# Cross-attention with a routed FFN on one core: loads after the output products, bias masks inside the weight sums, a new order at each group's start, a new opening

## The reference, cut to what matters

```python
x = x + xattn(layernorm(x), ctx, mask, bias, Wq, Wk, Wv, Wo)    # 1024 tokens of 512
x = x + ffn(layernorm(x))                  # dense product plus 8 routed rank-16 experts

def xattn(hq, hkv, mask, bias, Wq, Wk, Wv, Wo):  # 16 batches of 64 tokens, 32 heads of 128
    q, k, v = hq @ Wq, hkv @ Wk, hkv @ Wv        # 512 -> 4096 each
    score = q @ k.T / sqrt(128) + bias           # per batch and head, 64 x 64
    probs = softmax(where(mask, score, -inf))
    return (probs @ v) @ Wo                      # 4096 -> 512
```

## Time and profile before

| | |
|---|---|
| device time, median of three runs | 797.49 us (796.79 to 798.37) |
| profiled execution | 799.1 us, span 797.3 us |
| TensorE clock granted | 1.000 of full speed over the whole span |
| PE busy | 98% of the span |
| DVE, ACT, POOL busy | 73%, 42%, 23% |
| DMA engines | 148 GB/s on average, of queue q1 46.7% of 16 engines |
| chain that ended last | PE 89%, DVE 7%, DMA 2%, issue 1%, SP queue 1% |

### The profile page before, as it was taken

One profiled execution on the slowest core, in us unless ns is written; L12 is line 12 of the kernel. 1 busy time (PEld: TensorE's weight loads), 2 busy tenths in 40 slices (PEclk: granted clock), 3 DMA queues, 4 the chain that ended last, 5 costly groups with the idle time before them and its releaser, 6 DMA issues.

```text
span 797.3 us, 16339 instructions
## 1 busy us (share of the span) xinstructions
PE 781.9 (98%) x6368; PEld 651.8 (82%) x6368; DVE 585.0 (73%) x1047; ACT 335.4 (42%) x657; POOL 186.6 (23%) x203
## 2 busy tenths in 40 slices
PE   9999999999999999989999999999999999999998
PEld 7788888888888888768888878887888788888886
DVE  6794626267677666688987888788878887869884
ACT  5563525245455555452443234423443343324420
POOL 0134041024334334242212221212221221010200
PEclk9999999999999999999999999999999999999999
DMA  6536674234544556583564355435543455344002
GB/s 224 196 121 211 214 238 145 106 142 159 186 163 159 164 165 211 168 245 107 159 186 114 103 163 179 126 105 159 170 144 114 141 160 167 93 121 101 1 3 105
DMA packets 108075, 118.35 MB, mean 148 GB/s; under 512 B 44240, under 2 KB 77008, under 8 KB 107999
## 3 DMA queue, kind: packets, MB, share of 16 engines
q1 hardware_dynamic: 107998, 117.31, 46.7%
HBM read 81.64 MB, written 35.65 MB: 147 GB/s over the span
## 4 chain that ended last, share of the span: by engine, by line
PE 89%; DVE 7%; DMA 2%; issue 1%; SPq 1%; ACT 0%; DVEq 0%
PE pY L1383 40%; PE pP L1383 36%; PE pY L1544 4%; PE pO L1569 2%; PE pT_ L1569 1%; DVE pr L1140 1%; DVE rs L1135 1%; DVE y L1101 1%; DVE sm L1131 1%; PE pO L1383 1%; PE pT_ L1554 1%; PE pS L1554 1%; DMA k_hbm<-stage 1%; DMA v<-v_hbm 1%; SPq L422 1%
## 5 line engine op out<-in xcount | busy, mean ns | idle before, releaser
L1383 PE MATMUL pY<-wo_hi,oT_hi 128*128 128x512 f32 x248 | 97.8, 394 | 3.6 <-DVE y L1101 2.3
L1101 DVE TENSOR_TENSOR y<-y,pY 128x512 f32<-128x512 f32 x124 | 84.7, 683 | 18.6 <-PE pY L1383 18.3
L1383 PE MATMUL pY<-wo_lo,oT_hi 128*128 128x512 f32 x248 | 96.7, 390 | 0.0
L1383 PE MATMUL pY<-wo_hi,oT_lo 128*128 128x512 f32 x248 | 96.6, 390 | 0.0
L1383 PE MATMUL pP<-xo_hi,wk_hi 128*128 128x512 f32 x210 | 83.7, 398 | 1.8 <-ACT v_s L633 0.8
L648 ACT CAST wk_hi<-twk 128x256 fp32r<-128x256 f32 x128 | 52.1, 408 | 72.6 <-PE pP L1383 61.1
L1383 PE MATMUL pP<-xo_lo,wk_hi 128*128 128x512 f32 x210 | 81.9, 390 | 0.0
L1383 PE MATMUL pP<-xo_hi,wk_lo 128*128 128x512 f32 x210 | 81.9, 390 | 0.0
L581 POOL TENSOR_TENSOR bias<-bias,madd 128x512 f32<-128x512 f32 x32 | 42.7, 1348 | 151.8 <-DMA bias<-in_fside_Bx32xSxS 151.8
L887 DVE TENSOR_TENSOR wk_lo<-twk,wk_hi 128x256 fp32r<-128x256 f32 x128 | 58.8, 464 | 23.3 <-ACT wk_hi L648 23.3
L887 DVE TENSOR_TENSOR wk_lo<-wk_raw,wk_hi 128x256 fp32r<-128x256 f32 x96 | 46.6, 486 | 21.9 <-ACT wk_hi L648 21.8
(11 more groups left out here) (277 smaller groups left out, 1916.9 us busy)
## 6 DMA issues: line engine op xcount, KB each, us to landing
v_hbm<-stage SPq DMA_DIRECT2D x64, 256.0 KB, 2.3
k_hbm<-stage SPq DMA_DIRECT2D x64, 256.0 KB, 3.5
k<-k_hbm SPq DMA_DIRECT2D x16, 1024.0 KB, 5.4
v<-v_hbm SPq DMA_DIRECT2D x16, 1024.0 KB, 7.3
wk_raw<-in_L_xattn_Wk SPq DMA_DIRECT2D x16, 512.0 KB, 4.4
wo_raw<-in_L_xattn_Wo SPq DMA_DIRECT2D x16, 512.0 KB, 3.7
bias<-in_fside_Bx32xSxS SPq DMA_DIRECT2D x128, 64.0 KB, 3.5
wk_raw<-in_L_xattn_Wq SPq DMA_DIRECT2D x16, 512.0 KB, 4.6
```

Source lines behind the costliest of these rows:

```text
L1101: nc.vector.tensor_tensor(y[:, t, :], y[:, t, :], src[:, :], ALU.add).then_inc(y_added, 1)
L1383: mm = nc.tensor.matmul(bank_, a, b, start=first and n == 0, stop=last and n == len(terms) - 1, skip_group_check=read_between)
```

## The change

1. **Opening.** In `ORDER` product 5 of block 1 goes before product 2 of block 2. Two ACT copies keep the transposed context tiles 0 and 4 in SBUF (`kept0`), so the eight transposes that made them again in block 5 are gone, with one ACT copy (`rows_out(0)`). On ACT `higher(0, 4)` goes ahead of `copy_u(1)`, and `sums_high(2)` ahead of `copy_v(1)`; on DVE `first_low(2)` goes after `first_t1` and `first_t4`, and `sums_low(2)` ahead of `make_c11(2)`.
2. **The turn from K to the groups.** At block QA ACT's `copy_c12` goes before the first `exp`, and DVE's `make_c11` before the first `weights`.
3. **SP.** In each group, in place of wo, k, bias, Q weights, [v products done] v: wo, [v products done] Q weights, bias, k, v.
4. **POOL.** The two masks stand between the third and the fourth weight sum, not after the fourth.
5. **ACT and DVE in a group.** `wo_high` goes ahead of `higher` 3, and `lower_wo` goes from behind the fifth `add_tile` to behind the second.
6. **PE in a group.** `scores(h + 2)`, `turn_p(h)`, `scores(h + 3)`, `turn_p(h + 1)`, then both `times_v`.
7. **Tail.** PE's `ffn_weights(6)` goes after the products with V, and ACT's two `o_high` go ahead of `split_ffn(6)`.

Line numbers in the changed kernel are 5 to 15 higher in places: L1397 is the product, L1115 `add_tile`, L896 `lower`, L561 the mask, L571 to L584 the sums, L1553, L1563 and L1578 scores, transposes and products with V.

```diff
@@ -81,7 +81,7 @@
-ORDER = [(1, 1), (0, 2), (1, 2), (0, 4), (0, 3), (0, 7), (1, 6), (1, 7), (2, 1), (2, 2), (1, 5), (1, 3), (2, 6),
+ORDER = [(1, 1), (0, 2), (1, 2), (0, 4), (0, 3), (0, 7), (1, 6), (1, 7), (2, 1), (1, 5), (2, 2), (1, 3), (2, 6),
          (2, 7), (1, 4), (2, 5)]
...
@@ -91,10 +91,9 @@
-FIRST_TURN = [0, 1, 4, 6, 10, 12, 14, 16]
-SECOND_TURN = [2, 3, 5, 7, 11, 13, 15, 17]
-AGAIN = (8, 9)
-NTURN = 18
+FIRST_TURN = [0, 1, 4, 6, 8, 10, 12, 14]
+SECOND_TURN = [2, 3, 5, 7, 9, 11, 13, 15]
+NTURN = 16
...
@@ -510,15 +511,16 @@
                 load_wo(i + 1)
+
+                sp.wait_ge(o_full, 4 * (i + 1))
+                if i + 24 < NSET:
+                    load_wk(i + 24)
                 if i + 2 < NP:
-                    sp.wait_ge(s_full, 2 * i + 4)
-                    load_k(i + 2)
                     for s in range(2):
                         sp.wait_ge(s_read, 2 * i + 3 + s)
                         load_bias(2 * i + 4 + s)
-                if i + 24 < NSET:
-                    load_wk(i + 24)
-                sp.wait_ge(o_full, 4 * (i + 1))
+                    sp.wait_ge(s_full, 2 * i + 4)
+                    load_k(i + 2)
                 load_v(i + 1)
...
@@ -553,7 +555,12 @@
                 nc.gpsimd.tensor_tensor(rstd[:, b:b + 1], ve[:, b:b + 1], mhalf[:, :], ALU.pow).then_inc(rstd_made, 1)
-            def sums_of_b(w):
+            def add_mask(h):
+                pool.wait_ge(ld_bias[h % 2], 64 * (h // 2 + 1))
+                b = bias[h % 2]
+                nc.gpsimd.tensor_tensor(b[:, :, :], b[:, :, :], madd[:, :, :], ALU.add).then_inc(bias_made, 1)
+
+            def sums_of_b(w, masks=()):
...
@@ -570,15 +577,12 @@
                 nc.gpsimd.tensor_tensor(tw[:, 2, :, :], raw_block(w, 0, 1), raw_block(w, 0, 0), ALU.subtract
                                         ).then_inc(tw_made, 1)
+                for h in masks:
+                    add_mask(h)
                 pool.wait_ge(w_lo[6], w)
...
                                         ).then_inc(tw_made, 1)
-
-            def add_mask(h):
-                pool.wait_ge(ld_bias[h % 2], 64 * (h // 2 + 1))
-                b = bias[h % 2]
-                nc.gpsimd.tensor_tensor(b[:, :, :], b[:, :, :], madd[:, :, :], ALU.add).then_inc(bias_made, 1)
...
@@ -594,11 +598,12 @@
             for i in range(NP):
+                heads = (2 * i + 2, 2 * i + 3) if i + 1 < NP else ()
                 if i + 22 < NSET:
-                    sums_of_b(i + 22)
-                if i + 1 < NP:
-                    add_mask(2 * i + 2)
-                    add_mask(2 * i + 3)
+                    sums_of_b(i + 22, heads)
+                else:
+                    for h in heads:
+                        add_mask(h)
             pool.wait_ge(ld_small, 48)
...
@@ -655,7 +660,7 @@
             def rows_out(j):
-                act.wait_ge(turned, AGAIN[1] + 1 if j == 0 else SECOND_TURN[j] + 1)
+                act.wait_ge(turned, SECOND_TURN[j] + 1)
                 if j != 1:
...
@@ -697,15 +702,21 @@
             piece_of_first(1, 3, pP[0], c12_made)
+
+            act.wait_ge(a21_l, 1)
+            nc.scalar.copy(kept0[0][:, :, :, :], first_turn(0)[:, :].rearrange("p (k c t) -> p k c t", k=2, c=2)
+                           ).then_inc(kept0_made, 1)
+            nc.scalar.copy(kept0[1][:, :, :], second_turn(0)[:, :].rearrange("p (c t) -> p c t", c=DC)
+                           ).then_inc(kept0_made, 1)
             piece_of_first(3, 7, pP[1], c22_made)
             first_high(2)
+            higher(0, 4)
             copy_u(1)
             rows_out(2)
             last_high(2)
-            higher(0, 4)
             copy_p1(2)
+            sums_high(2)
             copy_v(1)
-            sums_high(2)
             higher(0, 6)
...
@@ -736,8 +747,6 @@
                 if j is not None:
                     sums_high(j)
-                if n == 5:
-                    rows_out(0)
                 copy_v(n)
...
@@ -792,8 +801,8 @@
             copy_v(n)
             higher(w, 4)
+            copy_c12(n)
             exp(0)
-            copy_c12(n)
             higher(w, 5)
...
@@ -831,10 +840,10 @@
                 copy_u(n)
                 higher_of(w, 2)
+                wo_high(i + 1)
                 higher_of(w, 3)
                 copy_v(n)
                 higher_of(w, 4)
-                wo_high(i + 1)
                 copy_c12(n)
...
@@ -854,9 +863,9 @@
             turned_p(h + 3)
             split_ffn(5)
-            split_ffn(6)
             o_high(h + 2)
             o_high(h + 3)
+            split_ffn(6)
...
@@ -925,7 +934,12 @@
                 low_, s, k = low[j // 4], sums_a[j // 4], SUM_ORDER.index(j)
                 one = first_turn(j)[:, :].rearrange("p (k c t) -> p k c t", k=2, c=2)
-                dve.wait_ge(low_made, k + 1)
+                if j == 0:
+                    one, low_ = kept0
+                    dve.wait_ge(kept0_made, 2)
+                else:
+
+                    dve.wait_ge(low_made, k + 1 if j < 4 else k)
                 if k >= 1:
...
@@ -1029,13 +1043,13 @@
             lower_w(0, 2)
             make_c11(1)
-            first_low(2)
             first_t1()
             first_t4()
+            first_low(2)
             lower_w(0, 4)
             sums_of_a(2)
+            sums_low(2)
             make_c11(2)
-            sums_low(2)
             lower_w(0, 6)
...
@@ -1180,9 +1194,9 @@
             add_up(0)
             lower_w(w, 6)
+            make_c11(n)
             weights(0)
             lower_w(w2, 0)
-            make_c11(n)
             add_up(1)
...
@@ -1217,6 +1231,7 @@
                 weights(h + 3)
                 add_tile(i, 1)
+                lower_wo(i + 1)
                 lower_of(w, 1)
...
@@ -1226,7 +1241,6 @@
                 lower_of(w, 5)
                 add_tile(i, 4)
-                lower_wo(i + 1)
                 add_tile(i, 5)
...
@@ -1436,8 +1450,7 @@
                 if j == 2:
-                    pe.wait_ge(a6_lo, 1)
-                    pe.wait_ge(a21_l, 1)
+                    pe.wait_ge(kept0_made, 2)
                 elif j == 4:
...
@@ -1499,8 +1512,8 @@
             times(1, 7)
             times(2, 1)
+            times(1, 5)
             times(2, 2)
-            times(1, 5)
             times(1, 3)
...
@@ -1514,10 +1527,6 @@
                 if prep_at(n) is not None:
                     turn_pair(prep_at(n))
-                if n == 5:
-                    pe.wait_ge(a6_lo, 3)
-                    turn(ctx[:, 0, :], first_turn(0))
-                    turn(ctx[:, 4, :], second_turn(0))
                 times(n, 6)
...
@@ -1637,10 +1646,10 @@
                 n = QA + 2 + i
                 h = 2 * i
+                scores(h + 2)
                 turn_p(h)
+                scores(h + 3)
                 turn_p(h + 1)
-                scores(h + 2)
-                scores(h + 3)
                 times_v(h)
...
@@ -1677,9 +1686,9 @@
             turn_p(h + 3)
             ffn_weights(5)
-            ffn_weights(6)
             times_v(h + 2)
             times_v(h + 3)
+            ffn_weights(6)
...
```

More of the change, by code:

```diff
@@ L201, in xattn_ffn @@
         sums_a = [at("sums_c", R2 + 2048, [P, 4, 2, P]), at("sums_x", R4 + 8192, [P, 4, 2, P])]
+        kept0 = [at("kept0_a", R2 + 6144, [P, 2, 2, P]), at("kept0_b", R2 + 8192, [P, DC, P])]
         R5 = R4 + 24576
@@ L287, in xattn_ffn @@
         turned, turned_hi, turned_lo = sem("turned"), sem("turned_hi"), sem("turned_lo")
-        low_made, sum_step = sem("low_made"), sem("sum_step")
+        low_made, sum_step, kept0_made = sem("low_made"), sem("sum_step"), sem("kept0_made")
         a01_hi, a01_lo, a6_hi, a6_lo = sem("a01_hi"), sem("a01_lo"), sem("a6_hi"), sem("a6_lo")
@@ L474, in _ @@
                     for t in range(NT):
-                        sp.wait_ge(turned, 10)
+                        sp.wait_ge(turned, 8)
                         sp.dma_start(y[:, t, :], x_d[:, t, :]).then_inc(ld_x[t], 16)
@@ L987, in normalise @@
                     if m >= NX:
-                        dve.wait_ge(turned, 10 + m - NX + 1)
+                        dve.wait_ge(turned, 8 + m - NX + 1)
                     nc.vector.tensor_scalar(xn[:, b, :], y[:, t, :], mv[:, b, 0:1], rstd[:, b:b + 1],
```

## The result

The changed kernel takes 806.32 us (median of four runs, 804.75 to 811.61) against 797.22 (796.79 to 798.37): a ratio of 1.0124, 95% interval 1.0073 to 1.0174. It is 9.1 us slower. The forecast was 800.0, slower but by 2.5, with a range that ended at 805.

The account below looks back on a forecast made before the run. PE was taken as the bound, busy for 98% of the span. Terms -2.8 - 0.2 + 4.2 - 2.7 + 4.4 - 0.4 = +2.5, added to the median 797.5, gave 800.0 us, with a range of 793 to 805.

Parts of the forecast that it names:

- the price of PE's order in the groups: Start of each group on PE: more changes between kinds of matmul cost 0.32 us a group, +4.2 in 13 groups.
- this order is hidden in the first group: First group after K: the new order is hidden behind the load of v, so it costs nothing there.
- what the fetches give back: Products with V: gaps are late instruction fetches costing 4.6 us; moved block ends leave 1.9, so -2.7.
- The masks with the low part of wo and the fourth sum: Groups: POOL's port lock delays DVE, so wo2 or wo4 stops 0.7 us a group; 9.1 less 4.7, +4.4.
- The opening's two stops: Opening: PE's stops for the v_s copy and co_lo go, -1.6 us of the opening's -2.8.
- the two stops near 336 and 341: From K to the groups: both go, worth 1.3 us together, but v's load takes the time back; -0.2 taken.
- The tail's stop for the low part of o: Tail, before 740.00: ACT's casts of o now stand ahead of one cast of 0.5, so -0.4 us.
- nothing to buy: Groups: scores 1.6 us earlier gain nothing, since no row of PE waits for the bias, exp or pT.
- (b): Groups: two locks in each group stop PE 1.15 us a group, +10.3; total 805.9 us, chance 0.12.
- (c): Products with V: the gaps stay, 0 and not -2.7; total 802.7 us, chance 0.13.
- (a): Groups: the masks fit, stops of 0.15 us or less, -2.7 in place of +4.4; total 792.9 us, chance 0.25.
- (d): Groups: PE's new order costs nothing, switches hidden in the halves; total 795.8 us, chance 0.10.

Follow-up runs that it names:

- e2: The changed kernel with DVE's low part of wo moved back behind the fifth y<-y,pY, as before: 799.38 us, ratio 1.0043 to the kernel before.
- e6: The kernel before with only PE's new group order: 799.74 us, ratio 1.0043.
- e5: The kernel before with 100 more semaphore instructions on PE ahead of its first one: 805.11 us, ratio 1.0115.
- e12: PE's new group order added to the kernel before with new opening, copies, tail, early low wo, later masks and 56 extra instructions: 796.19 us against 791.56.
- e1: The changed kernel with PE's group order as before (both transpositions, then both scores): 804.62 us, ratio 1.0095 to the kernel before.
- e4: The changed kernel with SP's load order as before (k, bias, Q weights, v): 804.04 us, ratio 1.0098 to the kernel before.
- e7: The kernel before with only the new opening, turn copies, earlier cast of wo's high part and new tail: 796.77 us, ratio 0.9991.

## Why the prediction was wrong, step by step

The time, 806.3, lies above the range of 793 to 805. Three steps failed: the price of PE's order in the groups (+4.2 forecast, +5.8 measured), the step that this order is hidden in the first group (0, and +1.6), and what the fetches give back (-2.7, and -0.8).

**Right in kind and near in size.** The bound was read rightly: PE, with DVE's y<-y,pY behind it. The masks with the low part of wo and the fourth sum were said to make 0.7 a group and +4.4; they made 0.72 and +5.1, with the stop at wo4, as said. That e2 takes nearly all of these stops away agrees with it. (The forecast's 7 x 1.36 + 0.1 for wo2 is 9.6, not 9.7; wo2 is due at 9.66, so nothing hangs on it.) The opening's two stops went, and the first scores, at 330.60 in the earlier trace rows, started at 328.19, 2.4 us earlier (2.8 forecast). Of the two stops near 336 and 341 only the second went; at 335.21 PE now waits 0.63 for DVE's copy. The tail's stop for the low part of o fell from 1.34 to 0.81, by the distance of the starts.

**The order of a group was mis-sized.** The term took 0.53 for four transposes behind scores, from a row where transposes come before; there it is 0.59, twice a group. So the term is +5.8, not +4.2, which is the very end that "0.12 more" gave. The sentence that there is nothing to buy was wrong: it looked only for waits of PE on the softmax, and not at what the scores release on SP. With the old loads the order takes nearly all stops at wo2 away (e6).

**The first group was not hidden.** The step that the new order in the first group is hidden behind the load of v failed. v landed at 348.44 and V started at 349.78, so v held nothing up (before, it landed at 351.17 and V started at 351.22). The second half of the first scores now waited 1.39 us for a copy of q that eight transpositions had covered before: +1.6 on the way to the first product of group 0.

**The fetches.** That the gaps are fetches stood and was shown (e5 and the packets). The size failed: -2.7 was forecast from the 13 groups and the first V alone, and the tail, which has two products with V beside the loads of the FFN's weights, was left out. There the shift by 16 put a gap of 2.0, so the total is -0.8 (4.6 before, 3.8 after; 5.0 and 3.9 by the lengths of the 16 products with V). Why this fetch came so late is open: its packet starts 0.8 behind the start of V (725.41, 724.60), while the one for the gap at 432.72 starts 0.2 ahead (430.22, 430.46). These three steps are 5.1 of the 6.0 us that the sum missed; the masks make 0.7 more.

**The rivals.** (b) gave the time, 805.9, by luck and not for its reason: the stops were as forecast, not 1.15 a group. (c) had a part of it. (a) fell: there are stops in all 13 groups. (d) fell too, by e12.

What stays open is how the spread of the changed kernel's runs (804.75 to 811.61) comes about. In e1 to e4 and e7 every execution with a mean granted clock of 0.998 or less is longer than all those at 1.000 of the same kernel. But the 811.61 has 0.998, which makes some 3 us at 0.50 and a loss of 1.6 us at most (an estimate from 0.002 x 810 / 0.5 and half of it), and the other three have 0.999 to 1.000. So the lower clock is a small part of it here, and the rest is not explained.
